# Two-layer graph attention with residual and LayerNorm on one core: where the window plans are read into registers, and how W1 arrives for the fold

## The reference

```python
h = (x @ W).reshape(N, H, C)
al_s = jnp.einsum('nhc,hc->nh', h, a_src)
al_d = jnp.einsum('nhc,hc->nh', h, a_dst)
e = jax.nn.leaky_relu(al_s[src] + al_d[dst], NEG_SLOPE)
m = jax.ops.segment_max(e, dst, num_segments=N)
ex = jnp.exp(e - m[dst])
denom = jax.ops.segment_sum(ex, dst, num_segments=N)
alpha = ex / (denom[dst] + 1e-16)
out = jax.ops.segment_sum(h[src] * alpha[:, :, None], dst, num_segments=N)
...
h = elu(gat(x, W1, 4 heads of 512, concatenated)); out = gat(h, W2, 1 head of 768)
return layernorm(x + out)
```

## Time and profile before

| What | Value |
|---|---|
| Median of 3 executions | 923.18 us (921.67 to 926.49) |
| Profiled execution, its own time | 924.97 us |
| Span of the profiled execution, first to last instruction | 922.9 us |
| Busy: PE, DVE, ACT, POOL | 873.8, 621.3, 422.2, 205.4 us |
| Mean granted TensorE clock over the span | 0.990 |

### The profile page before, as it was taken

One profiled execution on the slowest core, in us unless ns is written; L12 is line 12 of the kernel. 1 busy time (PEld: TensorE's weight loads), 2 busy tenths in 40 slices (PEclk: granted clock), 3 DMA queues, 4 the chain that ended last, 5 costly groups with the idle time before them and its releaser, 6 DMA issues.

```text
span 922.9 us, 15201 instructions
## 1 busy us (share of the span) xinstructions
PE 873.8 (95%) x5693; PEld 790.9 (86%) x5693; DVE 621.3 (67%) x1215; ACT 422.2 (46%) x681; POOL 205.4 (22%) x133
## 2 busy tenths in 40 slices
PE   4998879999999999999999999999999999999797
PEld 2456557799888998889988899989999999999796
DVE  8457663758893798937989279674122346797886
ACT  5356452166643676336664367853111111587300
POOL 1000000045322253222431234400000000154452
PEclk9999998999999999999999999999999999999899
DMA  8609897462576416774156534438123354050223
GB/s 299 149 15 135 174 183 147 150 167 94 187 252 186 147 48 202 236 198 136 48 164 215 133 127 136 128 121 193 51 73 67 70 76 99 1 121 9 76 83 93
DMA packets 71265, 119.72 MB, mean 130 GB/s; under 512 B 35660, under 2 KB 37352, under 8 KB 69818
## 3 DMA queue, kind: packets, MB, share of 16 engines
q1 hardware_dynamic: 71193, 118.76, 48.8%
HBM read 93.77 MB, written 24.96 MB: 129 GB/s over the span
## 4 chain that ended last, share of the span: by engine, by line
PE 69%; DVE 10%; issue 9%; POOL 6%; ACT 3%; DMA 1%; DVEq 0%; SPq 0%; POOLq 0%; ACTq 0%
PE ps L1831 19%; PE ps L1833 19%; PE ps L1832 19%; POOL pbuf L623 6%; PE ps L1860 4%; PE ps L1801 2%; PE ps L1952 2%; PE ps L1791 1%; DVE h2f L1738 1%; DVE pbuf L636 1%; DVE h2f L1712 1%; DMA w1f<-in_L_gnn_W 1%; DVE bnst L1729 1%; DVE vbuf L1495 1%; DVE vbuf L1494 1%
## 5 line engine op out<-in xcount | busy, mean ns | idle before, releaser
L623 POOL TENSOR_TENSOR pbuf<-pbuf,grow 125x625 f32<-125x625 f32 x99 | 177.4, 1793 | 680.9 <-ACT pbuf L608 244.3
L1831 PE MATMUL ps<-hx,PThi 125*125 125x260 f32 (+5 forms) x800 | 227.4, 284 | 2.8 <-DVE vbuf L1495 2.2
L1833 PE MATMUL ps<-hx,PTlo 125*125 125x260 f32 (+5 forms) x800 | 225.4, 282 | 0.0
L1832 PE MATMUL ps<-hlo,PThi 125*125 125x260 f32 (+4 forms) x800 | 224.9, 281 | 0.0
L1831 PEld LDWEIGHTS ps<-hx,PThi 125*125 125x125 f32 x800 | 148.7, 186 | 6.8 <-DVE vbuf L1495 2.7
L1832 PEld LDWEIGHTS ps<-hlo,PThi 125*125 125x125 f32 x800 | 149.1, 186 | 1.4
L1833 PEld LDWEIGHTS ps<-hx,PTlo 125*125 125x125 f32 x800 | 149.0, 186 | 0.0
L1831 PE MATMUL ps<-W2p,hT 128*125 128x384 f32 x320 | 109.9, 343 | 2.1 <-DVE vbuf L1495 2.1
L630 ACT ACTIVATE pbuf<-pbuf,s_sl 125x625 f32<-125x625 f32 x100 | 81.3, 813 | 59.1 <-POOL pbuf L623 57.0
L1833 PE MATMUL ps<-W2p,hT 128*125 128x384 f32 x320 | 108.1, 338 | 0.0
L1832 PE MATMUL ps<-W2p,hT 128*125 128x384 f32 x320 | 108.0, 338 | 0.0
(11 more groups left out here) (193 smaller groups left out, 1577.2 us busy)
## 6 DMA issues: line engine op xcount, KB each, us to landing
xr<-xT_scratch SPq DMA_DIRECT2D x30, 750.0 KB, 6.6
nbm<-mask_scratch SPq DMA_DIRECT2D x40, 273.4 KB
hidden_scratch<-vbuf SPq DMA_DIRECT2D x40, 224.0 KB
hblk<-hidden_scratch SPq DMA_DIRECT2D x10, 896.0 KB
xT_scratch<-xa SPq DMA_DIRECT2D x20, 375.0 KB, 10.5
w1f<-in_L_gnn_W SPq DMA_DIRECT2D x12, 512.0 KB, 9.5
w1raw<-in_L_gnn_W SPq DMA_DIRECT2D x4, 1536.0 KB, 7.3
wf<-in_L_gnn_W SPq DMA_DIRECT2D x16, 384.0 KB, 4.4
```

The source lines that it names most:

```text
L623: pool.tensor_tensor(pslot(c), pslot(c), src[:, g * GN:(g + 1) * GN], ALU.add).then_inc(e_done, 1)
L1831: pe.matmul(dst, ahi, bhi, start=start, stop=False, skip_group_check=shared)
L1832: pe.matmul(dst[:, 0:n], ahi, blo, start=False, stop=False, skip_group_check=shared)
L1833: return pe.matmul(dst, alo, bhi, start=False, stop=stop, skip_group_check=shared)
```

## The change

The number of plans that are read ahead, Q0, goes from 4 to 8, which is all of them, on PE and on DVE. On DVE all eight reads stand where four stood, ahead of the first window. On PE they no longer stand in one piece ahead of the fold: fold steps 0 and 1 come first, then the wait for `ranges` and plan 0, then step 2, plan 1, and so on to step 8, plan 7, and step 9. W1 for the fold is loaded in 8 transfers of 768 KB, two for each head, in place of 12 of 512 KB, six for each pair of heads, with a semaphore of its own for head 0, for head 1, and for heads 2 and 3 together.

```diff
-Q0 = 4
+Q0 = 8
...
-        ld_wf = [sem(f"ld_wf{i}") for i in range(2)]
+        ld_wf = [sem(f"ld_wf{i}") for i in range(3)]
...
-            for i in range(2):
-                for k in range(KD):
-                    sp.dma_start(w1f[:, 2 * i:2 * i + 2, k, :], W1[k * 128:(k + 1) * 128, 2 * i * HC:(2 * i + 2) * HC]
-                                 .rearrange("p (h c) -> p h c", h=2)).then_inc(ld_wf[i], 16)
+            for h in range(H):
+                for k in range(0, KD, KD // 2):
+                    sp.dma_start(w1f[:, h, k:k + KD // 2, :], W1[k * 128:(k + KD // 2) * 128, h * HC:(h + 1) * HC]
+                                 .rearrange("(k p) c -> p k c", p=128)).then_inc(ld_wf[min(h, 2)], 16)
...
-                    if i % (FU // 2) == 0:
-                        pe.wait_ge(ld_wf[i // (FU // 2)], 16 * KD)
+                    if i % (FU // H) == 0 and i // (FU // H) < 3:
+                        pe.wait_ge(ld_wf[i // (FU // H)], (32, 32, 64)[i // (FU // H)])
...
-            pe.wait_ge(ranges, 1)
-            ahead = [windows_plan(mybir.EngineType.PE, q) for q in range(Q0)]
+            ahead = []
             for i in range(FS):
                 fold_step(i)
+                if i == 1:
+                    pe.wait_ge(ranges, 1)
+                if 1 <= i <= Q0:
+                    ahead.append(windows_plan(mybir.EngineType.PE, i - 1))
```

## The result

The changed kernel takes 917.46 us (median of 7 executions, 914.85 to 919.72), the kernel before 925.66 (median of 7, 921.67 to 926.49). The ratio is 0.9926, 95% interval 0.9907 to 0.9945: 6.9 us less, with 5.1 to 8.6 by the interval (the two medians as they stand differ by 8.2). I had forecast 11.4 less. The span of the profiled execution went from 922.9 to 915.4, 7.5 less, and what lies behind the windows kept its distances, so the whole difference arises in the first 139 us.

A forecast was written before the change was run, and what follows sets the result against it. TensorE holds 69% of the chain, so only its waits pay; 3.2 + 0.4 + 1.4 + 4.4 + 1.6 + 1.2 = 12.2, less 0.8, leaves 11.4 us: median from 923.18 to 911.8, range 908.5 to 919.

The forecast's parts named there:

- rival B: Windows: waits at plans 5 and 6 stay without the reads; 7.2 us less or only 3.2, 916 to 920; chance 0.17.
- The start: Start of the fold: first product matmul at 15.1 in place of 18.5, set by ACT's copy; 3.2 us, 2.3 to 3.9.
- The eight reads between the fold steps: PE's fold: each 1.2 us read is covered by matmuls already handed on; cost 0, at most about 10 us.
- DVE's eight reads: Ahead of DVE's first window: four more reads end at 26, under cover of one-hot tiles lasting until 29.24; cost 0.
- Plans 4, 5 and 6: Windows 16, 20 and 24: waits at their reads go, plus half clock at window 24; 0.4, 1.4 and 4.4 us.
- Plan 7: Ahead of window 28: DVE's 1.77 us stand for the read goes, except its usual restart; 1.6 us.
- 1.2 of clock: Last two windows: half of the 2.4 us clock loss comes back; bounds 0 to 2.4.
- 0.8 for what comes late next: End of the windows: 0.8 us given back, 0 to 2, for busy DMA engines and ACT waiting for mask stores.
- a sign of being wrong: Between 125 and 140 us: ACT's masks waiting for stores would show the forecast wrong.

The follow-up runs named there:

- start alone: Changed kernel with Q0 = 4: four reads between fold steps, the other four again ahead of the later windows; 0.9970 of the kernel before.
- strip 5 first: Changed kernel with the store of mask strip 5 issued ahead of the store of the score rows; 0.9890 of the kernel before.
- strip 5 later: Changed kernel with the store of mask strip 5 moved behind the first mask loads and the xT stores of block 7; 1.0009 of the kernel before.
- copies sooner: Changed kernel with VectorE making all 20 groups of one-hot tiles and ACT none (LV, LA = 20, 0); 0.9901 of the kernel before.
- one-piece kernel: Changed kernel with PE's eight plan reads in one piece ahead of the fold; 1.0001 of the kernel before.
- reads alone: Changed kernel with W1's loads and waits as before (12 transfers, six a group), all eight plans still read ahead; 0.9936 of the kernel before.
- W1 alone: Kernel before with W1 loaded by head in 8 transfers, plan reads as before; 0.9996 of the kernel before.
- the control: Kernel before with only the store of mask strip 5 moved ahead of the score rows; 0.9971 of the kernel before.

## Why the prediction was right or wrong

The forecast was 11.4 us less, 911.8 in the base of then; it came to 6.9. The direction, and the reads as the cause, were right, but the size is too large by two thirds. The 917.46 lies in the stated range only because that was drawn on through rival B: the forecast's own bounds were 909 to 915, and rival B's band 916 to 920. That B's number was met is chance, since its mechanism, waits at plans 5 and 6 that stay without the reads, did not occur. Step by step, by the traces of before and of the changed kernel:

- *The start, 3.2 (2.3 to 3.9).* In the profiled execution window 0 came 2.0 earlier, under the lower bound. The first product matmul came 3.3 earlier, but from there to the transposes of step 3 it took 5.4 us (15.16 to 20.55) where before took 4.1 (18.47 to 22.57, its first line below), 1.3 of slower matmuls. In the four traces with this order of PE's queue (changed kernel, start alone, strip 5 first, strip 5 later) window 0 stands at 35.89, 35.74, 34.16 and 36.69, thus 1.2 to 3.8 earlier than 37.91. Over the executions of the start alone the gain is 2.8 (1.7 to 3.8) at the end of the program. So the term was right in kind and about 1 us large; that ACT, not W1, sets the first product matmul was read rightly, and copies sooner confirm it.

```profile
18.47 1.98 PE L1801 MATMUL ps<-wT,acz 128*8 128x384 f32 x4
```

- *The eight reads between the fold steps, 0.* Right. Steps of 2.19 in the trace, and the one-piece kernel shows what they cost without the cover.
- *DVE's eight reads, 0.* Right: DVE's first window at 29.17 in both.
- *Plans 4, 5 and 6: 0.4 + 1.4 + 4.4 = 6.2.* In the traces window 27 came 8.9 earlier, of which 2.0 are the start's: 6.9, by plan some 0.9, 1.7 and 4.2. Right, and rival B, in which the waits stay without the reads, is refuted: PE starts windows 20 and 24 without an idle time ahead of them.
- *Plan 7, 1.6 and 1.2 of clock, less "0.8 for what comes late next".* This is the step that failed. These three come to 2.0 more gain; from window 27 to the end of the windows the changed kernel lost 1.3 in place of it. From window 27's start to window 28's `ring` matmuls it took 7.3 us (6.2 before), and from there to the end 5.5 (5.3 before): neither plan 7's wait nor any of the clock came back. DVE was free for window 28 sooner, but what it needed, W1hi, stood behind the mask of strip 7 on ACT, and that waited 3.08 us for the store of strip 5. I had named that wait, also as a sign of being wrong, but priced it at 0.8, 0 to 2, without working out when each store lands. With the store first the same two stretches take 4.3 and 4.6 us, 2.6 less than before, near the 2.8 that the two terms (1.6 + 1.2) had promised. In sum, against the 11.4: 1.2 less at the start, 0.7 more at the plans, 3.3 less behind window 27, which makes 7.6 in the traces.

What was wrong inside that 0.8 can be read from SyncE's queue. I had written that the stores' work starts about 5 us earlier, after the score rows. The score rows did: their store was issued at 112.25 in place of 116.94. But SP waits for it to land before it goes on, and that took 4.8 us in place of 2.3, so that strip 5 was issued only 1.4 earlier. In the table are the starts in us ("SP goes on" is the first transfer behind the wait for the rows) and ACT's wait for the store ahead of strip 7:

| Kernel | Strip 4 issued | Rows issued | SP goes on | Strip 5 issued | Window 27 | ACT waits |
|---|---|---|---|---|---|---|
| before | 107.10 | 116.94 | 119.22 | 121.02 | 134.67 | 0 |
| start alone | 104.69 | 114.47 | 116.38 | 118.18 | 131.18 | 0 |
| changed kernel | 104.84 | 112.25 | 117.08 | 119.58 | 125.80 | 3.08 |
| reads alone | 106.27 | 114.10 | 118.34 | 120.14 | 127.63 | 2.27 |
| eight in one piece | 112.41 | 120.22 | 124.65 | 126.46 | 133.74 | 3.00 |
| copies sooner | 101.48 | 108.98 | 113.52 | 115.61 | 122.64 | 2.87 |

SP goes on 11.7 to 12.2 us after it issued strip 4's store, whenever the rows come. That store is issued ahead of PE's read of plan 5 (107.10 against 108.4 in the trace of before). So the gain at the start moves the stores too, and the gains of plans 5 and 6 don't: from the issue of strip 5 to window 27 there were 13.0 to 13.7 us with these reads in the windows and 6.2 to 7.5 without, and the store took 9.3 in the changed kernel. This fits the waits of all six, and why copies sooner kept its gain. It is read from the traces; no run moved strip 4's store to test it.

The error was to take "what is late next" as one small correction at the end of a sum, without asking which of the gains the next transfer shares. The chance that I gave to stores setting the end of the stretch lay inside rival B, tied to the wrong cause.

## What to carry to other kernels

A register read on an engine's queue costs its 1.2 us only where the engine has no work handed on; put it behind such work, not in a row ahead of the loop. When an edit moves a stretch by several microseconds, list each transfer that must land inside the stretch, with its issue and its landing after the edit, before adding up gains: a gain that comes ahead of the transfer's issue moves it along, one that comes behind it does not. Where a buffer's store waits on a queue behind other stores, its place in that queue can be worth as much as the edit itself: here from 0.9890 to 1.0009 for one store.

## What the runs showed of the hardware

- The same register read of PE took 1.2 to 1.4 us at the start, 3.6 to 3.8 ahead of window 24 in the kernel before, W1 alone and start alone, and 1.23 there when strip 5's store had been issued 6 us before it (the control). In those three it began 0.4 to 1.1 us behind the issue of a mask store. The early reads of the changed kernel, with W1 still streaming in, took 1.4 at most, and the last on each engine, which reads a plan of two windows in place of four, 0.74 and 0.75. That stores out of the core's memory lengthen a read is my reading of these; I didn't isolate it.
- The same matmuls ran at different speeds at the same place: the four at 15.16 took 2.72 us in the changed kernel's execution and 1.45 in that with strip 5 first, whose order there is the same. The granted clock reads 1.00 for both, so that the clock is behind it isn't shown. The second execution then lost 1 us between windows 10 and 11, in a stretch with a mean granted clock of 0.66 (second row), behind one with PE busy 2.62 us of 4 (first row):

```profile
66.00:70.00 4.00, 2.62 (x19) 1.00 0.02 4
70.00:74.00 4.00, 3.70 (x17) 0.66 1.05 187
```

So a microsecond or two at the start of one profiled execution says little; the ratios over several executions were needed.
